# Head outputs kept transposed, normalized by sums of P repeated on their partitions; routing weights written in two parts

## The reference

```python
# attention: 4 heads of 64; keys and values from the context and from the tokens themselves
xn = layernorm(ctx, ln_x_g, ln_x_b);  ln = layernorm(LN(x), ln_l_g, ln_l_b)
q = ln @ Wq.T;  kv = concat([xn @ Wkv.T, ln @ Wlkv.T], axis=1)        # 1601 + 2048 keys
attn = softmax(where(mask, (rmsnorm(q)*qn_g/8) @ (rmsnorm(k)*kn_g).T, -max))
x = x + (attn @ v) @ Wo.T + bo
# mixture of experts: 8 experts, the best 2 of each token, hidden width 512
z = LN(x);  probs = softmax(z @ router.T);  w, idx = top_k(probs, 2);  w = w/(sum(w)+1e-6)
x = x + sum_k w_k * ((silu(z @ w13_gate) * (z @ w13_up)) @ w2)[idx_k]
```

## Time and profile before

| | us |
|---|---|
| median of 3 runs | 1068.06 (1067.65 to 1069.13) |
| profiled execution | 1068.87 |
| its span | 1066.1 |
| PE busy | 957.3 (90%) |
| DVE busy | 711.4 (67%) |
| ACT busy | 484.2 (45%) |
| POOL busy | 567.5 (53%) |

### The profile page before, as it was taken

The page is one execution under the profiler, slowest core; times in us unless marked ns, Lnnn a source line. Parts: engine busy times, 40 slices in busy tenths (PEclk is TensorE's granted clock), DMA queues, the critical chain, the costliest instruction groups (busy, mean ns, idle before and its releaser), DMA issues.

```text
span 1066.1 us, 15449 instructions
## 1 busy us (share of the span) xinstructions
PE 957.3 (90%) x4544; PEld 622.9 (58%) x4545; DVE 711.4 (67%) x1418; ACT 484.2 (45%) x752; POOL 567.5 (53%) x437
## 2 busy tenths in 40 slices
PE   2699869999999999999999999999994299999994
PEld 1565535556555556556556656556544278888883
DVE  3889886776786776786776776776787244444542
ACT  0456625545555455555555655655552022332321
POOL 5130016776677666676766676676600145556552
PEclk9899968999999999999999999999997599999998
DMA  6010021121122221221222122121439753333332
GB/s 184 20 46 15 0 94 55 53 72 60 60 69 66 70 69 61 73 70 65 69 71 65 65 80 65 60 85 55 160 134 367 275 193 55 50 55 50 51 54 25
DMA packets 70610, 87.49 MB, mean 82 GB/s; under 512 B 12603, under 2 KB 66812, under 8 KB 68508
## 3 DMA queue, kind: packets, MB, share of 16 engines
q1 hardware_dynamic: 52046, 70.73, 18.8%
q0 software_dynamic: 7488, 10.39, 6.1%
q10 hardware_dynamic: 11022, 5.71, 1.9%
HBM read 50.03 MB, written 36.77 MB: 81 GB/s over the span
## 4 chain that ended last, share of the span: by engine, by line
PE 70%; DVE 6%; issue 4%; DMA 3%; ACT 2%; ACTq 0%; POOL 0%; POOLq 0%; DVEq 0%
PE bPV L1400 20%; PE bM L1320 10%; PE bS L1389 9%; PE bS L1390 8%; DVE mpart L972 2%; PE bG L1501 2%; PE bH L1518 2%; PE bY L1501 2%; PE bG L1503 2%; PE bG L1502 2%; PE bY L1503 2%; PE bY L1502 2%; PE bU L1503 2%; PE bU L1501 2%; PE bU L1502 2%
## 5 line engine op out<-in xcount | busy, mean ns | idle before, releaser
L972 DVE TENSOR_REDUCE mpart<-bM 128x1 f32<-128x464 f32 x492 | 295.4, 634 | 126.3 <-PE bM L1320 124.8
L492 POOL TENSOR_TENSOR acc_p<-acc_p,PT 128x1024 f32<-128x1024 f32 x120 | 302.6, 2521 | 104.2 <-ACT PT L751 100.7
L751 ACT ACTIVATE PT<-bS 128x1024 f32<-128x1024 f32 (+1 forms) x240 | 237.5, 997 | 199.8 <-PE bS L1390 171.4
L1400 PE MATMUL bPV<-PT,V 128*64 128x512 f32 x928 | 230.6, 604 | 0.0
L1389 PE MATMUL bS<-QQ,S 128*128 128x512 f32 x464 | 189.8, 409 | 3.2 <-ACT PT L751 0.8
L1320 PE MATMUL bM<-S,QQ 128*128 128x464 f32 x492 | 174.4, 414 | 11.5 <-DVE mpart L972 6.3
L1390 PE MATMUL bS<-QQ,S 128*128 128x512 f32 x464 | 183.8, 396 | 0.0
L1320 PEld LDWEIGHTS bM<-S,QQ 128*128 128x128 f32 x492 | 84.9, 191 | 94.9 <-DVE mpart L972 70.2
L496 POOL TENSOR_TENSOR wraw<-wraw,whi 128x256 fp32r<-128x256 f32 x96 | 85.2, 888 | 69.3 <-ACT whi L712 69.3
L1389 PEld LDWEIGHTS bS<-QQ,S 128*128 128x128 f32 x464 | 87.9, 190 | 55.0 <-issue 26.0
L1400 PEld LDWEIGHTS bPV<-PT,V 128*64 128x64 f32 x928 | 58.7, 136 | 104.4 <-issue 92.9
(11 more groups left out here) (232 smaller groups left out, 1480.9 us busy)
## 6 DMA issues: line engine op xcount, KB each, us to landing
W<-wsp_d SPq DMA_DIRECT2D x16, 1536.0 KB, 10.5
wraw<-w SPq DMA_DIRECT2D x96, 128.0 KB, 2.4
wsp_d<-whi SPq DMA_DIRECT2D x96, 128.0 KB, 2.4
wsp_d<-wraw SPq DMA_DIRECT2D x96, 128.0 KB, 1.7
V<-x SPq DMA_DIRECT2D x1, 2048.0 KB, 13.1
xb_d<-xbs SPq DMA_DIRECT2D x16, 128.0 KB, 1.7
x<-xb_d ACTq DMA_DIRECT2D x12, 128.0 KB, 2.0
out<-x ACTq DMA_DIRECT2D x12, 128.0 KB, 1.8
```

The costliest lines, as they stand in the source:

```text
L492: pool.tensor_tensor(acc_p[:], one, PT[:, q % NPT, :, :], ALU.add).then_inc(sem("z_p"), 1)
L751: act.activation(PT[:, p % NPT, 0:n, :], bS[(w.h + p) % 2][:, 0:n, :], ACT.Exp).then_inc(sem("exp"), 1)
L972: dve.tensor_reduce(mpart[:, i, g:g + 1], banks[k % len(banks)][:, 0:PIECE], AX, ALU.max)\
L1400: last = pe.matmul(bPV[b * D:(b + 1) * D, 0, :], V[:, c, h * D:(h + 1) * D], PT[:, p % NPT, b, :], start=c < 2, stop=c >= NK - 2, skip_gro ...
```

## The change

- The outputs stay transposed. o_copy copies one half of bPV onto the partitions of the other (64 partitions), DVE adds the other half (o_sum, at step 0), PE makes the sums of P already repeated on the head's 64 partitions with one matmul against a 128x64 tile of ones (z_rows, at step OUT_AT = 4), DVE inverts all 64x512 of them and multiplies straight into QT. o_T, heads_T, `on` and the copy at L691 go.
- The shares of the last five tiles are made mostly by POOL; the shares are stored in two DMAs (11 tiles at the end of the last unit, 5 later). The gathers wait for the stored rows and shares and for gidx; what concerns `out` is waited for by the first scatter.
- SP: loads of experts 4 and 3 come after the first two gathers have landed. The row comparisons of the first 11 tiles move from behind the last unit into it (steps 7 and 9). iot, til, rr and blk get bf16 forms for comparisons and products. Static scatters read sidx directly.

```diff
@@ sizes and types
+        onesd = sb("onesd", [P, D], at=small)            # instead of twin, orec, onec, on
+        iotb = sb("iotb", [P, P], BF16, at=t2)
-        til = sb("til", [P, 2 * NT], at=t2)
+        til = sb("til", [P, 2 * NT], BF16, at=t2)
-        rr = sb("rr", [P, 2, NT], at=t2)
+        rr = sb("rr", [P, 2, NT], BF16, at=t2)
+        ball = sb("ball", [P, 2 * NT], at=t2)
+        blk = sb("blk", [P, 2 * NT], BF16, at=t2)
@@ SP, behind load_w(2, 0), load_w(2, 1)
-            sp.wait_ge(sem("ox"), 16 * NF)
...
-            sp.sem_inc(sem("rows_out"), 1)
+            arrived(0)
+            arrived(1)
+            for k in range(2):
+                sp.wait_ge(sem(f"g_in{k}"), 16)
+            sp.wait_ge(sem("ox_t"), 16 * QB)
             load_w(4, 0)
             load_w(4, 1)
             sp.wait_ge(sem("r_sh"), 4)
             load_w(3, 0)
             load_w(3, 1)
-            arrived(0)
-            arrived(1)
-            for k in range(2):
-                sp.wait_ge(sem(f"g_in{k}"), 16)
             sp.wait_ge(sem("routed"), 1)
+            sp.wait_ge(sem("pad_out"), 16)
@@ POOL, constants
+                pool.tensor_copy(iotb[:], iot_i[:]).then_inc(sem("consts"), 1)
@@ POOL, ahead of the gathers
+            def shares_b():
+                sl, n = slice(NA, NT), NR
+                pool.wait_ge(sem("den"), 1)
+                pool.tensor_scalar(den[:, sl], den[:, sl], 1e-6, 1.0, ALU.mult, ALU.add).then_inc(sem("den"), 1)
+                pool.wait_ge(sem("den"), 2)
+                pool.tensor_tensor(den[:, sl], den[:, sl], ex[:, sl, E], ALU.add).then_inc(sem("den"), 1)
+                pool.wait_ge(sem("den"), 4)
...
+                pool.tensor_tensor(wd[:, sl, :], wd[:, sl, :], rb[:, sl, :], ALU.add).then_inc(sem("wd"), 1)
+            shares_b()
+            pool.wait_ge(sem("ol"), 16 * (NT - QB))
+            pool.wait_ge(sem("ol_t"), 16 * QB)
+            pool.wait_ge(sem("wd_out"), 32)
             pool.wait_ge(sem("gidx"), 1)
-            pool.wait_ge(sem("rows_out"), 1)
-            pool.wait_ge(sem("wd_out"), 16)
@@ POOL, scatter
                 if s.i is None and s.v == 0:
                     pool.wait_ge(sem("routed"), 1)
+                    pool.wait_ge(sem("ox"), 16 * (NT - QB))
+                    pool.wait_ge(sem("ox_t"), 16 * QB)
+                    pool.wait_ge(sem("pad_out"), 16)
...
+                if s.i is None:
+                    rows = sidx[:, s.v:s.v + 1]
+                else:
...                                                     # the copy into ring_s as before
@@ ACT
             def o_copy(n):
+                lo = (n - 1) % 2 * D
                 act.wait_ge(sem("pv"), NP * n)
-                if n > 1:
-                    act.wait_ge(sem("oT_a"), n - 1)
-                act.copy(oT_a[:], bPV[:, 0, :]).then_inc(sem("o_cp"), 1)
+                after(act, sem("o_ev"), n - 1)
+                act.copy(oT_a[lo:lo + D, :], bPV[D - lo:2 * D - lo, 0, :]).then_inc(sem("o_cp"), 1)
-            def heads_T(w): ...
+            def wd_store(lo, hi, n):                     # wd_store(0, NA, 1) ends the last unit
+                act.wait_ge(sem("wd"), n)                # wd_store(NA, NT, 2) stands where L798 stood
+                act.dma_start(xln_d[lo * P:hi * P, DIM:DIM + E].rearrange("(t p) e -> p t e", p=P), wd[:, lo:hi, :])\
+                    .then_inc(sem("wd_out"), 16)
@@ DVE
-            def o_out(n, h, gone): ...
+            def o_sum(n):                                # at p == 0
+                lo = (n - 1) % 2 * D
+                dve.wait_ge(sem("o_cp"), n)
+                dve.tensor_tensor(oT_a[lo:lo + D, :], bPV[lo:lo + D, 0, :], oT_a[lo:lo + D, :], ALU.add)\
+                    .then_inc(sem("o_sum"), 1)
+            def o_out(n):                                # at p == OUT_AT
+                b, h = divmod(n - 1, H)
+                k, lo = h // 2, h % 2 * D
+                dve.wait_ge(sem("z_mm"), n)
+                z = bT[lo:lo + D, 0, :]
+                dve.reciprocal(z, z).then_inc(sem("z_inv"), 1)
+                dve.wait_ge(sem("o_sum"), n)
+                dve.wait_ge(sem("z_inv"), n)
+                dve.tensor_tensor(QT[lo:lo + D, k, b * QW:(b + 1) * QW], oT_a[lo:lo + D, :], z, ALU.mult)\
+                    .then_inc(sem("o_ev"), 1)
@@ DVE, last unit and routing
+                if p in ROWS_A_AT:                       # in ahead(p)
+                    rows(A_, ROWS_A_AT.index(p))
...
-            rows(A_, 0)                                  # behind the units
-            rows(A_, 1)
...
+            dve.wait_ge(sem("r_ex"), 2)                  # ahead of ranks(B_, ...)
+            dve.tensor_reduce(den[:, B_], ex[:, B_, 0:E], AX, ALU.add).then_inc(sem("den"), 1)
...
+            dve.wait_ge(sem("den"), 3)                   # ahead of mov1
+            dve.reciprocal(wgt[:, 0, B_], den[:, B_]).then_inc(sem("den"), 1)
...
-            shares(B_, 2)
@@ PE
-            def o_T(n): ...
-            def heads_T(): ...
+            def z_rows(n):
+                lo = (n - 1) % 2 * D
+                pe.wait_ge(sem("zs"), n)
+                pe.matmul(bT[lo:lo + D, 0, :], onesd[:], acc_d[:, 0, :], start=True, stop=True)\
+                    .then_inc(sem("z_mm"), 1)
@@ PE, outputs
                     if p == 0:
-                        after(pe, sem("o_cp"), u)
+                        after(pe, sem("o_sum"), u)
@@ steps
-OUT_AT, HEADS_AT, Y_AT, SD_AT, X3_AT, X3T_AT, LG_AT = 5, 7, 8, 9, 10, 11, 12
+OUT_AT, Y_AT, SD_AT, X3_AT, X3T_AT, LG_AT = 4, 8, 9, 10, 11, 12
+ROWS_A_AT = (7, 9)
```

More of the change, by code:

```diff
@@ L407, in _ @@
             load_w(2, 1)
-            sp.wait_ge(sem("ox"), 16 * NF)
-            sp.wait_ge(sem("ol"), 16 * NF)
-            sp.wait_ge(sem("ox_t"), 16 * QB)
-            sp.wait_ge(sem("ol_t"), 16 * QB)
-            sp.wait_ge(sem("pad_out"), 16)
-            sp.sem_inc(sem("rows_out"), 1)
             def arrived(e):
@@ L571, in scatter @@
                 held()
-                pool.indirect_dma_start(out, bass.IndirectOffsetOnAxis(ap=ring_s[:, s.par:s.par + 1], axis=0),
+                pool.indirect_dma_start(out, bass.IndirectOffsetOnAxis(ap=rows, axis=0),
                                         ysb[:, s.par, :], None, compute_op=ALU.add)\
@@ L761, in unit @@
                         shares(slice(0, NA), 1)
-                    if p == HEADS_AT and w.h % 2 == 0 and not w.first:
-                        heads_T(w)
                     if p == SD_AT and w.fin:
@@ L772, in unit @@
                     c_row(v, w.next_h % 2)
+                else:
+                    wd_store(0, NA, 1)
             for k in range(2):
@@ L784, in _ @@
             o_copy(UNITS)
-            heads_T(Unit(NB, 0))
             NF = NT - QB
@@ L978, in maxima @@
                 dve.tensor_reduce(cmax[:], mpart[:], AX, ALU.max).then_inc(sem("cmax"), 1)
-            def o_out(n, h, gone):
-                dve.wait_ge(sem("oT_a"), n)
-                o = bT[:, 0, 0:QB * (D + 1)].rearrange("p (i d) -> p i d", i=QB)
-                dve.reciprocal(orec[:], o[:, :, D]).then_inc(sem("orec"), 1)
-                dve.wait_ge(sem("orec"), n)
-                if h % 2 == 0:
-                    after(dve, sem("oT_mm"), gone)
-                at = h % 2 * D
-                dve.tensor_tensor(on[:, :, at:at + D], o[:, :, 0:D],
-                                  orec[:].unsqueeze(2).to_broadcast([P, QB, D]), ALU.mult).then_inc(sem("o_ev"), 1)
+            def o_sum(n):
[13 more added lines that the diff above has]
+                    .then_inc(sem("o_ev"), 1)
             ND = len(DVE_SUMS)
@@ L1000, in z_sum @@
                 else:
-                    after(dve, sem("oT_a"), w.u)
+                    after(dve, sem("z_mm"), w.u)
                 dve.wait_ge(sem("exp"), NP * w.u + max(p, q) + 1)
@@ L1110, in unit @@
                 for p in range(NP):
+                    if p == 0 and not w.first:
+                        o_sum(u)
                     if p == OUT_AT and not w.first:
-                        o_out(u, (w.h - 1) % H, w.pairs)
+                        o_out(u)
                     for n, at in enumerate(LAST_AT if w.last else DVE_AT):
@@ L1145, in _ @@
             run_units(unit)
-            o_out(UNITS, H - 1, None)
-            rows(A_, 0)
-            rows(A_, 1)
+            o_sum(UNITS)
+            o_out(UNITS)
             NF = NT - QB
@@ L1327, in c_T @@
                 last.then_inc(sem("cT_mm"), 1)
-            def o_T(n):
-                pe.wait_ge(sem("o_cp"), n)
+            def z_rows(n):
+                lo = (n - 1) % 2 * D
                 pe.wait_ge(sem("zs"), n)
-                for i in range(QB):
-                    at = i * (D + 1)
-                    pe.matmul(bT[:, 0, at:at + D], oT_a[:, i * P:(i + 1) * P], twin[:], start=True, stop=True)
-                    last = pe.matmul(bT[:, 0, at + D:at + D + 1], acc_d[:, 0, i * P:(i + 1) * P], onec[:],
-                                     start=True, stop=True)
```

(19 more changed lines are left out.)

48 lines of the change are left out of this document (21 added, 27 removed).

## The result

The changed kernel takes 1142.13 us (median, 1141.03 to 1145.42, four runs) against 1068.12: ratio 1.070, interval 1.0686 to 1.0712. The direction was forecast, the size was not: the forecast was 1115 us, and 1142 lies outside its range of 1095 to 1134. The profiled execution took 1141.98 us, its span is 1140.2 (before 1066.1).

What follows compares the result with a forecast made beforehand. TensorE was taken to bound the units (39.96 us busy of 40.54). 1068.9 - 14.4 (work) + 49 (stall) + 17 (clock) - 7.2 (last unit, gather) + 3 (contention) = 1116.3, less 0.8: 1115 us, range 1095 to 1134.

Steps and rivals of the forecast that it cites:

- The clock: Units 1 to 14: TensorE's clock falls behind the stall in ten units, 1.7 us each, +17 us; bounds 0 and 24.
- Work taken from TensorE: Units 1 to 14: o_T and heads_T go, z_rows comes at 0.85 us each, -14.4 us in sum.
- The stall: Units 1 to 14: TensorE waits 3.5 us at the second piece of p=5 behind VectorE's divide, +49 us.
- The price of the divide: VectorE's reciprocal of 512 in o_out: 3.35 us, from forms of 4, 8 and 16; bounds 0.69 and 3.6.
- Last unit and projection: VectorE bounds the last unit; divide and row comparisons bring the first projection about 5.1 us later.
- Routing and first gather: Gather waits for gidx, not the shares' store, and starts at 834.2: -7.2 us together with the last unit.
- Contention: First expert blocks: held back loads meet scatters, two or three blocks lose some time, +3 us, bounds 0 and 8.
- A: Rival: the reciprocal streams at a sum's rate, 0.69 us, stall 0.9 us per unit: 1057 us, faster; chance 0.08.
- B: Rival: TensorE's clock holds through the stall in the units: 1098 us; chance 0.18.
- C: Rival: the divide costs the skill page's 4.4 us: 1132 us; chance 0.07.
- D: Rival: shares' store stays slow or held weights cost their upper bound, tail gains nothing: 1122 to 1127 us; chance 0.1.

Runs made afterwards that it cites:

- no divide: The changed kernel with the reciprocal of 64x512 replaced by an instruction of the same shape that writes a constant: 1068.07 us, ratio 0.9999.
- divide in three parts: Kernel before with only the transposed outputs and their normalization, sums two steps earlier, reciprocal and product in thirds between pieces: 1064.45 us, ratio 0.9972.
- routing part alone: Kernel before with only the routing, shares, gather and load order, row comparisons in the last unit: 1072.66 us, ratio 1.0049.
- the repaired kernel: Whole change with split divide, comparisons in gaps: loads of experts 4 and 3 early 1062.58 us; only 4 early, 3 behind the gathers 1060.61 us.

## Why the prediction was wrong

**The clock: the step that failed.** I gave it 10 x 1.7 = 17 us, with 24 as the upper bound; it measures 30, by two kernels. Both factors were too small. The clock fell in all fourteen units, not ten. And in six of them it stayed low much longer than the 3.4 us that I read off the window 802 to 808, one place with short matmuls and gaps. In windows of half a microsecond eight units (mean clock 0.96 in their rows) show 3.4 us at half speed and six (0.92 or 0.93) 6.8 us, part of it inside the stall, where it costs nothing. In the six the clock falls 0.6 to 1.1 us before the stall ends; in the eight it falls between 0.3 us before that and 1.5 us after it. Why this decides the length, no run shows. My "upper bound" counted falls but kept the length fixed.
The trace of before had a longer fall, which I missed: I read nines at full clock from the fifth slice on, but the clock digits of the sixth and seventh slice are 6 and 8. Behind an idle gap of 5.03 us that ends at 139.46, the clock is down from about 138.2 to 145.1, 6.8 us again, and 5.6 of them are TensorE's work (windows as above, kernel before):

```profile
138.00:140.00 2.00, 0.54 (x2) 0.56 0.12 38
140.00:142.00 2.00, 2.00 (x7) 0.50 0.20 70
142.00:144.00 2.00, 2.00 (x7) 0.50 0.19 66
144.00:146.00 2.00, 1.93 (x5) 0.73 0.60 197
```

That in all fourteen units would have made an upper bound of 14 x 2.8 = 39 us.
The Trainium skill (TensorE: Matmul & The Clock Gate, HAM oscillation — how this bites in real kernels) was right against my ten: by it a recurring wait inside the matmul work lets the clock down every time, and every unit here shows it.

**Work taken from TensorE: mis-sized.** -14.4 forecast, -6.8 and -5.7 measured (no divide; divide in three parts). z_rows was priced as the fifth chunk of a run of chunks. Alone among matmuls of another form it costs more: scores run 0.23 us apart with a piece of 0.21 between, while here from the score at 749.99 to the one behind z_rows and a piece at 751.65 it is 1.66 us, so z_rows takes 1.66 - 0.23 - 0.21 = 1.22 us, not 0.85. That is 5.2 of the missing 7.6 to 8.7 us. The rest is not placed; pieces behind the stall start 0.1 to 0.2 us late, below what the idle column lists, and no run isolates that.

**The stall: right.** 14 x 3.5 = 49 forecast, 46.5 measured as additional idle time in the units (53.2 less 6.7), nearly all at the piece and behind the releaser named (3.23 of 3.81 us in unit 13). The price of the divide was right too: 3.35 forecast from forms of 4, 8 and 16 elements, 3.37 measured, and 1.25 for 171. The Trainium skill (VectorE: DVE Perf Modes, First, the fixed hardware budget) leads to an estimate of 4.4 us; the measurement decides for the rows.

These three make the units' error: +46.5 of stall instead of +49, +30 of clock instead of +17, -7 instead of -14.4, which is +69.4 against +51.6. The whole fell 27 us too low, and the clock is the largest term of it (13), then the work (8), the blocks (6) and the last unit (3); with the clock alone put right it would have been 1128 us.

**Last unit and projection.** +8.2 against +5.1. The summing of costs on VectorE was right as far as it went; its last sum of P ends 43.7 us after unit 14, 7.2 later than before, where I had 4.4. What it left out is that VectorE's delay comes back to it as waits of its own (2.5 us here, 2.1 in the routing part alone), since layer norm, projection and the last sums alternate between the engines.

**Routing and first gather.** -11.6 against -12.3, and the gather waits for gidx as forecast. The reason given was half right: I credited the smaller store and the held loads together. The runs credit the held loads with 11.4 us, all the rest with 0.2. The five tiles' store took 1.9 us, not 4.4. (Expert 2, too, is wanted later than the 885 us that I wrote: ten blocks of 5.7 us from 844.4 end at 901. Nothing hung on it.)

**Contention.** +3, bounds 0 and 8, against +8.7 (10.2 in the routing part alone), beyond the upper bound. I counted two or three blocks that lose some of a 6.57 us scatter; beside twice the load a scatter takes 10.00 and a gather 9.34 us, and each stands in the chain. In these waits the clock falls as well, which I had not priced: 0.83 from 930 to 950 us, while the kernel before has 1.00 from 860 on.

**The rivals.** A (the reciprocal streams) did not happen, but its arithmetic was tested: the stall "about eats the 14.4 us saved", and in the kernel without a divide it is 9.3 us and eats the 6.8 that are really there, for 1068 us where A said 1057. B (the clock holds) is refuted by every unit. C is refuted by 3.37 us. D (the tail gains nothing) came true by another road: the gather gained its 11.6 us, the projection and the blocks took back 8.2 and 8.7.

## What to carry to other kernels

An instruction of 3.4 us placed whole in front of a two-deep buffer stopped the engine behind it for 3.3 us, however idle its own engine is on average; cut in thirds and put between the buffer's items, the same work stopped nobody (ratio 1.068 against 0.997). Before a behaviour of the clock is priced from one place of a trace, look for all the others that the trace has. Price a recurring stall on TensorE as its length plus the clock that it costs behind it, here 3.3 + 2.1 us a unit, and count it in every unit. When a transfer is made early by holding others back, look for where the held ones go: here 11.4 us at the gather cost 8 in the blocks in one kernel and 10.5 cost 10.8 in another, with no gain in the kernel's time; holding half of them gained 2 us in the repaired kernel.

## What the runs showed of the hardware

- A reciprocal on VectorE costs 6.2 to 6.5 ns for each further element of a partition, from 4 elements up to 512 (178 ns for 4, 1.25 us for 171, 3.37 us for 512); a product of 512 takes 0.69.
- A stall of TensorE of 3.2 to 3.8 us in otherwise full matmul work let its clock fall to 1.2 GHz in each of fourteen units, for 3.4 us in eight and 6.8 us in six, the six in which it fell 0.6 us or more before the stall ended. The fourteen falls cost 30 us beyond the stalls.
- Matmuls whose result nobody reads, put into a stall of 3.3 us, keep the clock at 2.4 GHz and made this kernel 25 us faster than the same kernel without them.
- While weights are loaded at a DMA share of 1.0, a store of 20 KB in pieces of 32 B takes as long (13.68 us) as one of 64 KB (14.18); with fewer loads ahead of it 5.67, and with the loads held back the 64 KB take 3.0.
- Two comparisons of 1408 elements, each against a value repeated along the row, take 3.15 us together, with bf16 operands as with float32 ones.
